# int8 weights turned to fp16 by GpSimd's transfers in a windowed-attention and FFN kernel

## What is computed

```python
x = x + layernorm(attention_block(layernorm(x), qkv_w, conv..., proj_w, proj_b, ln_w, ln_b))
x = x + layernorm(ffn(layernorm(x), w_gate, w_up, w_down, s_gate, s_up, s_down))

def attention_block(x, ...):
    tok = x.reshape(B, H * W // 16, 16)
    q, k, v = split(tok @ qkv_w)
    # two branches of 8 channels; windows of 8 tokens along a row or along a column
    o = softmax(q @ k.T * scale) @ v + depthwise_conv3x3(v)
    att = concat(o1, o2) @ proj_w + proj_b
    tok = tok + layernorm16(att) * ln_w + ln_b
    return transpose(tok, (0, 2, 1)).reshape(B, H, W)

def ffn(x, ...):                      # w_gate, w_up (512, 2048), w_down (2048, 512), all int8
    gate = silu((x @ w_gate) * s_gate)
    up = (x @ w_up) * s_up
    return ((gate * up) @ w_down) * s_down
```

## Time and profile before

| | |
|---|---|
| median of 3 runs | 983.97 us (980.8 to 984.06) |
| the profiled execution | 981.15 us |
| its span, first to last instruction | 979.4 us |
| first `gate` starts at | 110.8 us |
| PE, DVE, ACT, POOL busy | 93%, 88%, 67%, 78% of the span |

### The profile page before, as it was taken

How to read it: one execution, slowest core, us unless ns; L and a number is a source line. 1 busy time by engine, 2 the same in 40 slices (tenths; PEclk the granted TensorE clock), 3 DMA queues, 4 the chain that set the end, 5 groups by cost and what they waited for, 6 DMA issues and landing times.

```text
span 979.4 us, 17776 instructions
## 1 busy us (share of the span) xinstructions
PE 908.9 (93%) x6527; PEld 705.8 (72%) x6527; DVE 863.2 (88%) x1088; ACT 660.3 (67%) x1151; POOL 761.2 (78%) x709
## 2 busy tenths in 40 slices
PE   4645799999999999999999999999999999999996
PEld 3534777878777777778777777777777777777774
DVE  5999999999999999999999999999999999993322
ACT  2778686767777676768677686867768585645332
POOL 3687688887889888888889888787987888777323
PEclk9867899999999999999999999999999999999998
DMA  5613130222203012221303212130302011111101
GB/s 120 195 43 77 31 84 4 66 65 53 78 23 108 23 44 65 66 65 33 98 23 71 57 46 65 44 88 1 93 16 63 25 44 44 45 43 44 45 1 44
DMA packets 68886, 54.94 MB, mean 56 GB/s; under 512 B 40384, under 2 KB 56768, under 8 KB 68800
## 3 DMA queue, kind: packets, MB, share of 16 engines
q1 hardware_dynamic: 63936, 53.49, 20.6%
q10 hardware_dynamic: 4864, 0.32, 0.3%
HBM read 37.02 MB, written 16.78 MB: 55 GB/s over the span
## 4 chain that ended last, share of the span: by engine, by line
PE 65%; DVE 13%; POOL 7%; issue 6%; ACT 5%; DMA 1%; ACTq 1%; POOLq 0%; DVEq 0%
PE ps_up L574 17%; PE ps_gate L574 16%; PE ps_acc L593 16%; PE ps_w L535 8%; DVE xr L1071 5%; DVE prod L993 3%; PE ps_w L555 3%; DVE fst L1076 2%; POOL sum L851 2%; PE ps_w L526 2%; PE ps_w L565 2%; PE ps_w L544 1%; DMA xr<-in_L_attn_x 1%; POOL frs L802 1%; ACT o L719 1%
## 5 line engine op out<-in xcount | busy, mean ns | idle before, releaser
L851 POOL TENSOR_TENSOR sum<-prod 128x1024 f32<-128x1024 f32 x128 | 302.2, 2365 | 41.8 <-DVE prod L993 31.3
L993 DVE TENSOR_TENSOR prod<-ps_x,qkvl 128x2048 f32<-128x2048 f32 x128 | 290.3, 2279 | 2.4 <-ACT ps_x L687 1.9
L593 PE MATMUL ps_acc<-wd,mid 128*128 128x512 f16 x1024 | 241.4, 379 | 0.0
L574 PE MATMUL ps_up<-xhi,wu 128*128 128x256 f16 x1024 | 230.6, 273 | 1.5 <-DVE mid L1094 1.5
L574 PE MATMUL ps_gate<-xhi,wg 128*128 128x256 f16 x1024 | 230.5, 273 | 0.0
L574 PE MATMUL ps_gate<-xlo,wg 128*128 128x256 f16 x1024 | 230.5, 273 | 0.0
L574 PE MATMUL ps_up<-xlo,wu 128*128 128x256 f16 x1024 | 230.5, 273 | 0.0
L755 ACT ACTIVATE mid<-ps_gate,sgate 128x256 f32<-128x256 f32 x256 | 106.7, 467 | 125.6 <-PE ps_gate L574 125.3
L919 POOL TENSOR_TENSOR mid<-mid 128x512 f16<-128x512 f32 x128 | 154.7, 1209 | 36.1 <-ACT mid L761 36.1
L593 PEld LDWEIGHTS ps_acc<-wd,mid 128*128 128x128 f16 x1024 | 100.2, 98 | 96.6
L1094 DVE SCALAR_TENSOR_TENSOR mid<-ps_up,sup,mid 128x256 f32<-128x256 f32 x256 | 110.6, 473 | 52.0 <-PE ps_up L574 43.7
(11 more groups left out here) (140 smaller groups left out, 1336.4 us busy)
## 6 DMA issues: line engine op xcount, KB each, us to landing
xrow<-in_L_attn_x SPq DMA_DIRECT2D x16, 512.0 KB, 3.7
xb<-in_L_attn_x SPq DMA_DIRECT2D x128, 64.0 KB
attn_rows<-ratt SPq DMA_DIRECT2D x32, 256.0 KB, 2.6
o<-attn_rows SPq DMA_DIRECT2D x32, 256.0 KB, 3.5
xr<-in_L_attn_x SPq DMA_DIRECT2D x16, 512.0 KB, 5.0
out_x<-y SPq DMA_DIRECT2D x15, 512.0 KB, 4.1
mid<-in_L_ffn_w_gate SPq DMA_DIRECT2D x1, 1024.0 KB, 5.6
mid<-in_L_ffn_w_up SPq DMA_DIRECT2D x1, 1024.0 KB, 8.1
```

Of the source, the lines that this page charges most:

```text
L574: mm = nc.tensor.matmul(ps[:, ROWS * i:ROWS * i + ROWS], w[:, k, P * j:P * j + P], xs[:, n % 2, k, :], start=(k == 0 and part == 0), stop= ...
L593: return nc.tensor.matmul(ps_acc[q][:], f[:, m % SPLITS, ROWS * i + P * q:ROWS * i + P * q + P], wd[:, 2 * m + i, :], start=(m == 0 and pa ...
L851: nc.gpsimd.tensor_tensor(sum4[:, u % 2, :].rearrange("p (s c) -> p s c", c=4), s[:, :, 0:4], s[:, :, 4:8], ALU.add).then_inc(half_done, 1)
L993: nc.vector.tensor_tensor(prod[:, half].rearrange("p (s j k) -> p s j k", j=WIN, k=WIN), left[:, :, None, :].broadcast_to([P, 4 * WIN, WIN ...
```

## The change

The three loads by SyncE and the 12 casts by ScalarE are gone, with the semaphore `w_cast` and the use of `mid` and `xr` as staging buffers. GpSimd issues 12 transfers in their place, which read int8 from HBM and write fp16 into `wg`, `wu` and `wd`: eight of 128 rows of 2048 elements (gate and up), and four of 4x128 rows of 512 elements (down). They are counted by weight; TensorE waits for each weight where it first uses it. SyncE's first two loads of `xr` wait for no cast any more. `START`, `PLAN` and `OWN` hold other numbers and another order. The set of steps ahead of the first `gate` stays the same but for two on the loads' side: `load_row 6` stands later and `att_store 1` earlier, and the row statistics of tile 5 stand at the prologue's end now.

```diff
-                if n < 2:
-                    sp.wait_ge(w_cast, CASTS)
                 sp.dma_start(xr[:, n % 2].rearrange("p q n -> p (q n)"), x_ffn[n // 4, n % 4]).then_inc(s_xr[n % 2], 16)
...
-            def load_weights(n, *_):
-                for dst, w, loaded in zip(staged, (w_gate, w_up, w_down), s_wload):
-                    rows = w.shape[0] // P
-                    sp.dma_start(dst.bitcast(I32).rearrange("p (k n) -> p k n", k=rows),
-                                 w.rearrange("(k p) n -> p k n", p=P)).then_inc(loaded, 16)
...
             def gate(n, m, bank):
                 if n == 0 and m == 0:
-                    pe.wait_ge(w_cast, CASTS)
+                    pe.wait_ge(s_wload[0], 16 * KB)
                     pe.wait_ge(scales_set, 1)
...
             def up(n, m, bank):
+                if n == 0 and m == 0:
+                    pe.wait_ge(s_wload[1], 16 * KB)
...
             def down(n, m, bank):
                 pe.wait_ge(flo_done, CHUNKS * n + m + 1)
+                if n == 0 and m == 0:
+                    pe.wait_ge(s_wload[2], 16 * KB)
...
-            def cast(n, i, bank):
-                w, k = i // KB, i % KB
-                if k == 0:
-                    act.wait_ge(s_wload[w], 16)
-                part = slice(k * INTER, k * INTER + INTER)
-                dst = (wg[:].rearrange("p k n -> p (k n)"), wu[:].rearrange("p k n -> p (k n)"),
-                       wd[:].rearrange("p m n -> p (m n)"))[w]
-                nc.scalar.activation(dst[:, part], staged[w].bitcast(I8)[:, part], ACT.Copy).then_inc(w_cast, 1)
...
+            def cast(n, i, bank):
+                w, k = i // KB, i % KB
+                if w < 2:
+                    dst, src = (wg, wu)[w][:, k], (w_gate, w_up)[w].bitcast(I8)[P * k:P * k + P]
+                else:
+                    dst = wd[:, KB * k:KB * k + KB]
+                    src = w_down.bitcast(I8)[KB * P * k:KB * P * k + KB * P].rearrange("(m p) n -> p m n", p=P)
+                pool.dma_start(dst, src).then_inc(s_wload[w], 16)
...
-        PLAN = [(-150.00, ("load_row",)), (-119.88, ("stats",)), (-108.21, ("load_xb",)), (-106.52, ("spread",)),
+        PLAN = [(-139.26, ("load_row",)), (-120.20, ("stats",)), (-107.95, ("load_xb",)), (-106.77, ("spread",)),
```

More of the change, by code:

```diff
@@ L36 @@
 LATER = 9
-CASTS = 3 * KB
 SETUP_POOL = 3
@@ L278, in runs @@
             return True
[L280 to L308, removed]
@@ new lines, in sandwich_kernel @@
+        PLAN = [(-139.26, ("load_row",)), (-120.20, ("stats",)), (-107.95, ("load_xb",)), (-106.77, ("spread",)),
+                (-96.66, ("apply",)), (-78.16, ("xt", 0, 0)), (-76.33, ("xt", 0, 1)), (-68.10, ("qkv", 0, 0)),
+                (-65.44, ("qkv", 0, 1)), (-65.39, ("xt", 1, 0)), (-62.50, ("qkv", 0, 2)), (-62.21, ("qkv", 0, 3)),
+                (-61.13, ("qx", 0)), (-60.96, ("qkv", 1, 0)), (-60.33, ("qkv", 1, 1)), (-58.18, ("xt", 1, 1)),
+                (-56.71, ("token_bias",)), (-56.69, ("qkv", 1, 2)), (-54.08, ("qkv", 1, 3)), (-49.87, ("qk", 0)),
+                (-48.87, ("qk", 1)), (-48.03, ("qk_sum", 0)), (-47.34, ("qx", 1)), (-46.88, ("qk", 2)),
+                (-46.46, ("qk_sum", 1)), (-45.95, ("qk", 3)), (-45.94, ("softmax", 0)), (-44.08, ("qk_sum", 2)),
+                (-41.77, ("exp", 0)), (-40.94, ("qk_sum", 3)), (-39.59, ("pv", 0)), (-37.15, ("pv", 1)),
+                (-35.95, ("exp", 1)), (-34.75, ("pv_sum", 0)), (-34.75, ("softmax", 1)), (-34.17, ("pv_sum", 1)),
+                (-33.81, ("pv", 2)), (-33.14, ("pv", 3)), (-29.81, ("pv_sum", 2)), (-28.64, ("pv_sum", 3)),
+                (-27.83, ("att_store",)), (-27.55, ("attn_out",)), (-26.04, ("recip",)), (-24.00, ("cat", 0)),
+                (-23.96, ("cat", 1)), (-22.83, ("proj", 0)), (-22.56, ("load_xr",)), (-21.97, ("square", 0)),
+                (-21.08, ("proj", 1)), (-20.50, ("cent_var",)), (-18.56, ("square", 1)), (-18.10, ("cent_std",)),
+                (-17.71, ("cent_out",)), (-10.73, ("ffn_norm1",)), (-6.38, ("norm1_add",)),
+                (-5.84, ("ffn_norm2",)), (-3.67, ("norm2_apply",)), (-1.86, ("fx", 0)), (-1.14, ("fx", 1)),
+                (7.11, ("keep_x1",)), (33.48, ("finish",)), (35.41, ("finish_apply",)), (35.57, ("finish_add",))]
@@ L792, in _ @@
                   "norm2_apply": norm2_apply, "keep_x1": keep_x1, "fx": fx, "gate": gate, "fuse_hi": fuse_hi,
[L793 removed]
+                  "finish_apply": finish_apply, "finish_apply_last": finish_apply_last})
         @block.gpsimd
@@ L943, in _ @@
                                     pattern=[[C, WIN + 2]], channel_multiplier=-1).then_inc(tokens_done, 1)
-            walk({"stats": stats, "scales": scales, "token_bias": token_bias, "qk": qk, "pv": pv, "attn_out": attn_out,
+            walk({"stats": stats, "scales": scales, "cast": cast, "token_bias": token_bias, "qk": qk, "pv": pv, "attn_out": attn_out,
                   "cent_out": cent_out, "ffn_norm1": ffn_norm1, "ffn_norm2": ffn_norm2, "finish": finish,
```

150 lines of the change are left out of this document (84 added, 66 removed), and 13 rows, old and new, of the table OWN.

## The result

The changed kernel takes 991.88 us (median of 4 runs, 990.85 to 993.4), the kernel before beside it 984.01 (980.8 to 984.23): the ratio is 1.0089, 95% interval 1.0063 to 1.0115. It is slower by 0.9%, where 978 was forecast. The profiled execution took 993.4 us, its span is 991.6.

The account below looks back on a forecast made before the run. VectorE was taken to bound the prologue and TensorE the tiles. 2.7 us from the prologue and 3.4 from the tiles' ends make 6.1 us less, 978 us against the runs' median of 983.97; range 971 to 993.

Parts of the forecast that it names:

- What bounds the kernel: Whole kernel: VectorE bounds the prologue, with 3.10 us idle; TensorE bounds the tiles, idling 0.54 us in a middle one.
- The casts: Prologue: taking twelve casts off ScalarE frees VectorE's waits, 1.21 + 0.95 us less, bounds 0 and 3.10.
- The start: Before VectorE's first product: constant matmuls now follow the fourth qkv step, 0.5 us less, at most 1.11.
- The transfers on GpSimd: Prologue: seven issues of 1.2 us each fit into GpSimd's idle time, 1.45 us per place, and cost 0.
- if VectorE waits for GpSimd in the prologue: One of the signs in the changed kernel's profile by which the prediction would be wrong.
- Rivals 2 and 3: Prologue bound by GpSimd's issues (993 at 3.6 us each, chance 0.13); conversion makes w_down's transfers slow (993, chance 0.06).
- The rule that the prediction set against the change: GpSimd-issued transfers would wait for VectorE's copy or one-source multiply under way; a us at most on the sum.
- When the weights land: From the prologue's end: w_down's transfers are hidden up to 8 us each; 2.6 to 3.2 us estimated until landing.
- The end of each tile: Middle tiles: the next gate starts 0.26 us earlier, 3.4 us for 13 tiles, bounds 7.0 us either way.
- Lock-outs: Prologue: VectorE and GpSimd holding each other up, counted 0 of a range from -1.7 to +1.7 us.
- The sum: Whole kernel: 2.7 us from the prologue plus 3.4 from the tiles, 6.1 us less, forecast 978.
- Rival 4: Tiles: the new order is worse by 0.54 us each, a wait for VectorE; 988.3 us, chance 0.04.

Follow-up runs that it names:

- e16: Changed kernel with PLAN's token_bias moved from -56.71 to -60.72; 983.16 us, ratio 1.0010.
- e17: e16 with the old places of tiles 14 and 15, but for their row loads, statistics and spread; 974.64 us, ratio 0.9924.
- e15: e4 with spread of tile 14 at 232.90, and in START the first qk of tile 1 ahead of attn_out of tile 0; 985.59 us.
- e7: e2 with five of the twelve transfers moved later, one of up and four of down; 984.76 us, ratio 1.0024.
- e4: Changed kernel with PLAN and OWN from the kernel before, START and transfers as changed; 984.14 us, ratio 1.0023.
- e2: Kernel before with all its tables of order, only the weight transfers put on GpSimd where the casts stood; 991.78 us, ratio 1.0087.
- e12: e4 with spread of tile 14 at 232.90, and each of the twelve transfers issued as two halves; 983.90 us, ratio 1.0021.
- e6: Changed kernel with the old places for every step of tiles 14 and 15; 984.02 us, ratio 1.0020.
- e3: Changed kernel with cent_out of tile 15 moved from place 341.88 to 344.50; 991.75 us, ratio 1.0095.
- e9: Changed kernel with only the attention steps of tiles 14 and 15 at their old places; 991.79 us, ratio 1.0096.
- e10: Changed kernel with every step of tiles 14 and 15 but the attention's at its old place; 1018.56 us, ratio 1.0369.
- e13: Changed kernel with tile 15's cat to cent_out 3 places later; 992.56 us, ratio 1.0099.

## Why the prediction was wrong

- **What bounds the kernel** was right for the tiles: TensorE's idle time was to be had there, and e16 and e17 had it. The stretch behind the first `gate`, forecast at 865 us, took 878.4 in the changed kernel (991.6 - 113.2). For the prologue it was half: VectorE is full, but the way of tile 0's attention ends at the same time. e15 took one wait of 2.65 us from VectorE and got one of 6.66 for that way.
- **"The casts", 1.21 + 0.95 us less: failed.** The wait of 1.21 us for ScalarE is gone, and these came in its stead, in VectorE's timeline of the changed kernel:

```profile
69.06 2.29 DVE L986 TENSOR_TENSOR prod<-ps_x,qkvl 128x2048 f32<-128x2048 f32 x1 [2.64 <-POOL sum L844]
...
73.91 1.22 DVE L1033 TENSOR_REDUCE cvar<-catt 128x64 f32<-128x1024 f32 x1 [1.42 <-ACT catt L701]
...
110.51 0.69 DVE L1076 TENSOR_TENSOR xlo<-ps_w,xhi 128x512 f16<-128x512 f32 x1 [0.86 <-ACT xhi L729]
```

  From VectorE's first product to `norm1_add` it is 72.1 us in the kernel before (26.20 to 98.28), 72.2 in e7, which has the old order without casts (28.06 to 100.24), and 72.1 in e4, with the new order (24.80 to 96.95). In e7 the wait of 1.21 us is gone as well, but VectorE's waits for GpSimd's sum and for `catt` grew from 0.45 and 1.01 us to 1.03 and 1.84. So taking the casts off ScalarE and putting the issues on GpSimd are worth 0 together; no run has one without the other, so the worth of each alone is not shown. The first `gate` came at 113.23, not at 108. By the timelines it started 13.7 us behind `norm1_add` in the changed kernel and 13.4 in e4, 12.4 before: the new order loses 1 us there too.
- **"The start", 0.5 us: not refuted.** The first product began 1.4 us earlier in e4's trace, at 24.80 us, and at 24.6 to 26.2 in all 17 traces with this start (26.20 before, 28.0 and 28.1 in e2 and e7). In the changed kernel's own trace it gained nothing (26.2): the 16 qkv products ahead of it took 5.55 us, 4.21 in e4.
- **"The transfers on GpSimd", covered: right for the length of an issue, too simple for its cost.** 0.54 to 0.85 us each for 1.2 forecast. But the cover is thin: e12's doubling cost 2.0 us where the step would have said 0 up to 1.45 us per place, so the first twelve may cost something too. The prediction's sign "if VectorE waits for GpSimd in the prologue" did come, the 2.64 us above (0.45 before). What stands ahead of that sum is `attn_out` of tile 0, 4.5 us, and not a long issue; e15 took the wait away and gained nothing. Rivals 2 and 3 fell: no issue came near 2.3 us, and no weight came late. The rule that the prediction set against the change (the Trainium skill's page "SBUF — State Buffer", section "SBUF: two separate sides") would show as issues held up by VectorE; none took over 0.85 us. The rule was hardly put to the test: no copy of VectorE stood beside an issue, and the one-source multiplies beside the two at 16.2 us (1.23 us together) were short, 0.92 us for three.
- **"When the weights land": right here, and incomplete.** 3.8 to 5.5 us at the median. The Trainium skill's page "DMA: Bandwidth & Descriptors", section "Anatomy of one DMA", gave an estimate of 2.6 to 3.2 us; the measurement decides, and it is above. What the step left out is the other direction: what these transfers do to those beside them. At the old places that was most of e2's 10 us; in the changed kernel the reordered prologue keeps them apart.
- **"The end of each tile", 0.26 us less for 13 tiles: the step that failed in the middle.** The wait for ScalarE went, as walked through. But the walk starts behind `norm1_add` and so took it with its old length, and the new table puts GpSimd's `xl` beside it: 0.66 us longer per half, 55.9 us per tile instead of 55.5. That belongs to "Lock-outs", where I had counted 0 with a range of 1.7 us for the prologue and nothing for the tiles. The new order was worth 0.7 us per tile (55.8 to 55.1) and gave it all away by one entry.
- **The sum had no term for tiles 14 and 15: the step that failed at the end.** "For the 13 tiles from the first to the last but two" left them out; `OWN` writes them anew, entry by entry, and they cost 12.6 us between the two traces. Ahead of tile 13 the same new places gain: from tile 0 to tile 13 the changed kernel takes 715.6 us, e6 721.1. So e6 gives back 7.9 in all. Rival 4 had the right kind of cause, a worse order in the tiles, but at 0.54 us for each tile and with a chance of 0.04.
- **The sign** is wrong by these two together. Without the tail's cost (e6) the ratio to before is 1.0020, without the lock-out (e16) 1.0010, without both (e17) 0.9924. e17's gain of 7.2 us on its own runs of before is near the forecast 6.1, but that is luck: it comes from the tiles, and nothing of it from the casts. It is luck too that 991.9 lies under the range's upper end: the range reached to 993 for rivals 2 and 3.

Which single entry of the tail costs is not settled. e3, e9, e10 and e13 exclude the simple answers: it isn't `cent_out`'s place, nor the stall behind tile 15's ends, nor either half of the steps alone. How the new places of tiles 14 and 15 make the late attention costly stays open.
